# A four-layer cross-attention kernel: key norms by a power on GpSimd, idle products in an attention, and expert gate and up products in halves

## The reference, cut to what matters

```
# layer 1 (the second), attention, per head, window of 64 keys back
scores = q . k ; e = exp(scores - max) ; ctx = (e / sum(e)) @ v ; out = ctx @ o_w.T + o_b
# layer 1, feed-forward: 16 routed experts and a shared one (as two more), n = 448 tokens
gu   = einsum('nc,ech->neh', xf, gate_up_w)       # 128 -> 128 gate, 128 up
h    = silu(gate) * up
out  = einsum('neh,ehc->nec', h, down_w)          # 128 -> 128
moe  = einsum('ne,nec->nc', w_full, out)          # top 2 of 16, sigmoid gates
# layer 2 (the third), attention: keys of 1500 context rows, 8 heads of 64
k = k / max(sqrt(sum(k*k)), 1e-12) * k_scale
```

## Time and profile before

| | |
|---|---|
| median of 3 runs | 826.67 us (825.04 to 827.05) |
| the profiled execution, its own time | 825.94 us |
| its span | 824.1 us |
| granted TensorE clock, mean over the span | 0.943 |
| TensorE busy | 735.4 us (89%) |
| VectorE busy | 615.2 us (75%) |
| ScalarE busy | 438.3 us (53%) |
| GpSimd busy | 347.0 us (42%) |

### The profile page before, as it was taken

The page is one execution under the profiler, slowest core; times in us unless marked ns, Lnnn a source line. Parts: engine busy times, 40 slices in busy tenths (PEclk is TensorE's granted clock), DMA queues, the critical chain, the costliest instruction groups (busy, mean ns, idle before and its releaser), DMA issues.

```text
span 824.1 us, 15426 instructions
## 1 busy us (share of the span) xinstructions
PE 735.4 (89%) x5468; PEld 469.1 (57%) x5468; DVE 615.2 (75%) x1297; ACT 438.3 (53%) x739; POOL 347.0 (42%) x283
## 2 busy tenths in 40 slices
PE   3799999997886978998899999998899999898997
PEld 3577787776544465663455555563346666653443
DVE  4779999998878765567565566658689999516786
ACT  2656667677484433435444545432127776743674
POOL 0665555561523501640677787740242211102464
PEclk8999999999998878999999999999859999999999
DMA  8267767532424512206022333007736678101520
GB/s 208 75 205 252 252 198 227 173 117 72 98 67 131 160 51 76 86 29 177 3 79 78 104 100 101 6 10 103 128 71 131 124 126 165 37 2 64 180 78 12
DMA packets 50645, 89.71 MB, mean 109 GB/s; under 512 B 17427, under 2 KB 34779, under 8 KB 50099
## 3 DMA queue, kind: packets, MB, share of 16 engines
q1 hardware_dynamic: 50578, 88.83, 39.8%
HBM read 63.29 MB, written 25.52 MB: 108 GB/s over the span
## 4 chain that ended last, share of the span: by engine, by line
PE 29%; DVE 17%; POOL 2%; ACT 2%; issue 2%; DVEq 0%; POOLq 0%; ACTq 0%
DVE arena L2516 11%; PE ps L1165 9%; PE ps L1155 7%; PE ps L1334 3%; PE ps L1348 2%; DVE arena L1898 2%; POOL arena L1820 2%; PE ps L1270 2%; PE ps L1259 1%; ACT arena L1647 1%; PE ps L1201 1%; PE ps L1242 1%; PE ps L1313 1%; PE ps L1171 1%; PE ps L768 1%
## 5 line engine op out<-in xcount | busy, mean ns | idle before, releaser
L2516 DVE TENSOR_REDUCE arena<-ps 112x1 f32<-112x500 f32 x192 | 114.6, 670 | 9.0 <-PE ps L1242 9.0
L1820 POOL TENSOR_TENSOR arena<-arena 125x448 f32<-125x448 f32 x96 | 109.2, 1137 | 24.6 <-ACT arena L1606 20.7
L1898 DVE TENSOR_TENSOR arena<-ps,arena 128x448 f32<-128x448 f32 (+7 forms) x139 | 80.8, 612 | 37.5 <-ACT arena L1564 18.3
L1647 ACT ACTIVATE arena<-ps 125x896 f32<-125x896 f32 x96 | 87.2, 917 | 23.5 <-PE ps L1259 23.4
L1165 PE MATMUL ps<-arena 125*128 125x448 f32 (+1 forms) x208 | 97.2, 548 | 2.0 <-ACT arena L1606 1.5
L1606 ACT ACTIVATE arena<-arena,kbias 125x448 f32<-125x448 f32 x96 | 63.6, 668 | 65.4 <-DVE arena L1898 47.9
L1898 DVE TENSOR_TENSOR arena<-ps,rn 125x448 f32<-125x448 f32 x96 | 59.2, 618 | 47.0 <-PE ps L1155 42.1
L843 PE MATMUL ps<-w_k2h,arena 128*125 128x512 f16 x288 | 69.4, 392 | 11.6 <-ACT arena L1416 10.4
L1155 PE MATMUL ps<-arena 128*125 128x448 f16 (+3 forms) x312 | 76.5, 354 | 1.2 <-DVEq L1909 1.1
L1155 PEld LDWEIGHTS ps<-arena 128*125 128x125 f16 (+1 forms) x312 | 40.1, 133 | 54.8 <-issue 41.8
L1416 ACT ACTIVATE arena<-ps 125x512 f32<-125x512 f32 x96 | 55.4, 598 | 12.4 <-PE ps L843 9.8
(11 more groups left out here) (323 smaller groups left out, 1462.7 us busy)
## 6 DMA issues: line engine op xcount, KB each, us to landing
arena<-in_ctxT SPq DMA_DIRECT2D x8, 750.0 KB, 9.3
d_cln<-arena SPq DMA_DIRECT2D x8, 750.0 KB
d_clnT<-arena SPq DMA_DIRECT2D x8, 750.0 KB
d_k<-arena SPq DMA_DIRECT2D x24, 250.0 KB
d_v<-arena SPq DMA_DIRECT2D x24, 250.0 KB
arena<-d_clnT SPq DMA_DIRECT2D x8, 750.0 KB
arena<-in_ctx SPq DMA_DIRECT2D x8, 672.0 KB
arena<-d_cln SPq DMA_DIRECT2D x8, 672.0 KB
```

The lines of the kernel that those rows point to most:

```text
L1647: act.activation(p3[t % 2].rearrange("p (k h) q -> p k (h q)", k=2), ps[0:KP, 2 * (t % 2):2 * (t % 2) + 2, 0:8 * S], ACT.Exp).then_inc(l3_ ...
L1820: ins = pool.tensor_tensor(psum2[p][0:rows], psum2[p][0:rows], pexp[(t + p) % 2][0:rows], ALU.add)
L1898: return dve.tensor_tensor(out, a, b, op)
L2516: dve.tensor_reduce(mx3[bn % 2][:, u % 2, u % 8 // 2, u // 8:u // 8 + 1], ps[0:TT, max_bank_of(bn, u), 0:500], AX.X, ALU.max).then_inc(l3_ ...
```

## The change

**Norms.** The square root on ScalarE and the reciprocal on VectorE go. In their place GpSimd raises all of `rn` to the power -0.5 in one instruction, between `remainders(22)` and `remainders(23)`. VectorE waits for it (`rn_rt`) just before the third layer's attention.

**Idle products.** Before `turn_probs1(3)` TensorE waits until VectorE has read the last scores and then issues `keep_clock(9, 1)`.

**Experts.** Gate and up products are made of halves: `wh1` holds the high part and the remainder of the six gate and up matrices of a group, `x1h` those of the activations. The casts of groups 0 and 1 stand on ScalarE before `probs1(3)`, the subtractions on VectorE behind `normalise1(3)`; those of groups 2 to 5 stand in the expert stage, once in three experts. Both parts of `x1h` are made after `xT`, ahead of the first gate product. `gate_up1` now runs two experts ahead of `down1`, with three PSUM pairs and three `ex1` and `h1` tiles. The weights of a group are laid out as all gates and ups, then all downs, and loaded in two transfers, of 384 and 192 KB, each as its part of the buffer is free. All loops of this stage are written out. The waits of the fourth layer on the shared semaphores are shifted by what the second layer now adds to them (`SPLITS1`, and three down loads for each buffer).

```diff
+GU1 = G1 * 2 * 128
+SPLITS1 = 7
...
+UP_BANKS1 = (3, 5, 1)
...
+        wh1, h1, ex1 = [], [xT2, xT3], [exs[0], exs[1]]
+        for p in range(2):
+            words = kblk[p].rearrange("p e h s -> p (e h s)")
+            wh1.append(words[:, 0:768].bitcast(F16).rearrange("p (w n) -> p w n", w=2))
+            (h1, ex1)[p].append(words[:, 768:768 + N])
+        x1h = kblk[0].rearrange("p e h s -> p (e h s)")[:, 768 + N:768 + 2 * N].bitcast(F16).rearrange("p (w n) -> p w n", w=2)
...
-            def load_experts1(g, p):
-                sp.dma_start(wex[p][:, 0:G1 * 3 * D], batch(io["L1_ex"], g)).then_inc(ex_ld[p], 16)
+            def load_gate_up1(g, p):
+                sp.dma_start(wex[p][:, 0:GU1], io["L1_ex"][g, :, 0:GU1]).then_inc(ex_ld[p], 16)
+
+            def load_down1(g, p):
+                sp.dma_start(wex[p][:, GU1:G1 * 3 * D], io["L1_ex"][g, :, GU1:G1 * 3 * D]).then_inc(ex_ldd[p], 16)
...
-            with sp.Fori(0, E1 // G1 // 2 - 1) as i:
-                for p in range(2):
-                    g = 2 * i + p
-                    sp.wait_ge(ex_dn, G1 * (g + 1))
-                    load_experts1(g + 2, p)
+            sp.wait_ge(ex_split, 2)
+            for p in range(2):
+                load_gate_up1(2 + p, p)
+            for g in range(E1 // G1 - 2):
+                sp.wait_ge(ex_dn, G1 * (g + 1))
+                load_down1(g + 2, g % 2)
+                if g + 4 < E1 // G1:
+                    sp.wait_ge(ex_split, g + 4)
+                    load_gate_up1(g + 4, g % 2)
...
             for i in range(NT):
+                if i == NT - 1:
+                    pe.wait_ge(l1_sr, NT)
+                    keep_clock(9, 1)
                 turn_probs1(i)
                 if i + 2 < NT:
...
-            def w1(k, group, col):
-
-                return wex[group][:, D * (3 * k + col):D * (3 * k + col) + D]
-
-            def gate_up1(s, loads):
-
-                if s % G1 == 0:
-                    pe.wait_ge(ex_ld[s // G1 % 2], 16 * loads)
+            def gate_up1(e):
+
+                g, at = e // G1, e % G1 * 2 * D
+                pe.wait_ge(ex_split, 3 if g < 2 else g + 2)
+                if e > 2:
+                    pe.wait_ge(ex_h, e - 1)
                 for m in range(2):
-                    mm = pe.matmul(ps[0:D, 2 + 2 * (s % 2) + m, 0:N], w1(s % G1, s // G1 % 2, m), xT,
-                                   start=True, stop=True)
+                    for n, (w, a) in enumerate(((0, 0), (0, 1), (1, 0))):
+                        mm = pe.matmul(ps[0:D, UP_BANKS1[e % 3] - 1 + m, 0:N], wh1[g % 2][:, w, at + D * m:at + D * m + D],
+                                       x1h[:, a, :], start=(n == 0), stop=(n == 2))
                 mm.then_inc(ex_gu, 1)
...
-            def expert1(turn, s, more=True):
-                e = 2 * G1 * turn + s
-                if more:
-
-                    pe.wait_ge(ex_h, e + 1)
-                    gate_up1(s + 1, turn + 1 + (s + 1) // (2 * G1))
+            def down1(e):
+                g = e // G1
+                if e % G1 == 0:
+                    pe.wait_ge(ex_ldd[g % 2], 16 * (g // 2 + 1))
                 pe.wait_ge(ex_w, e + 1)
                 pe.wait_ge(ex_h, e + 2)
+                at = GU1 + e % G1 * D
                 for t in range(NT):
-                    mm = pe.matmul(ps[0:TT, 6 + s % 2, D * t:D * t + D],
-                                   (xT2, xT3)[s % 2][:, TT * t:TT * t + TT], w1(s % G1, s // G1 % 2, 2),
-                                   start=True, stop=True)
+                    mm = pe.matmul(ps[0:TT, 6 + e % 2, D * t:D * t + D], h1[e % 3][:, TT * t:TT * t + TT],
+                                   wex[g % 2][:, at:at + D], start=True, stop=True)
                 mm.then_inc(ex_dn, 1)
 
-            gate_up1(0, 1)
+            gate_up1(0)
             pe.wait_ge(lk_taken, 24 - IN_TURNS)
             pe.wait_ge(lv_taken, 24 - IN_TURNS)
-            with pe.Fori(0, E1 // (2 * G1) - 1) as i:
-                for s in range(2 * G1):
-                    expert1(i, s)
-            for s in range(2 * G1):
-                expert1(E1 // (2 * G1) - 1, s, more=s < 2 * G1 - 1)
+            gate_up1(1)
+            pe.wait_ge(to_act, 1)
+            for e in range(E1):
+                if e + 2 < E1:
+                    gate_up1(e + 2)
+                down1(e)
...
-            act.wait_ge(rn_sq, 1)
-            rn_flat = rn[:, :, :, :].rearrange("p b t h -> p (b t h)")
-            act.activation(rn_flat, rn_flat, ACT.Sqrt).then_inc(rn_sd, 1)
...
+            def split_hi1(g):
+                act.wait_ge(ex_ld[g % 2], 16 * (g // 2 + 1))
+                if g > 1:
+                    act.wait_ge(ex_gu, G1 * (g - 1))
+                act.copy(wh1[g % 2][:, 0, :], wex[g % 2][:, 0:GU1]).then_inc(ex_hi, 1)
+
             for i in range(NT):
+                if i == NT - 2:
+                    act.wait_ge(l1_s, NT)
+                    split_hi1(0)
+                    split_hi1(1)
...
+            act.wait_ge(operand, OPERAND["latentsT"] - 2)
+            act.copy(x1h[:, 0, :], xT).then_inc(ex_hi, 1)
+
+            def silu1(e):
                 act.wait_ge(ex_gu, e + 1)
-                act.activation(exs[p], ps[0:D, 2 + 2 * p, 0:N], ACT.Silu).then_inc(ex_act, 1)
-
-            silu1(0, 0)
-            silu1(1, 1)
-            act.wait_ge(to_act, 1)
-            act.activation(sm16[:, 6], sm16[:, 0], ACT.Sigmoid).then_inc(from_act, 1)
-            with act.Fori(1, E1 // 2) as i:
-                for p in range(2):
-                    silu1(2 * i + p, p)
+                act.activation(ex1[e % 3], ps[0:D, UP_BANKS1[e % 3] - 1, 0:N], ACT.Silu).then_inc(ex_act, 1)
+
+            for e in range(E1):
+                silu1(e)
+                if e == 1:
+                    act.wait_ge(to_act, 1)
+                    act.activation(sm16[:, 6], sm16[:, 0], ACT.Sigmoid).then_inc(from_act, 1)
+                if e % G1 == 0 and 1 < e // G1 + 1 < E1 // G1:
+                    split_hi1(e // G1 + 1)
...
-            remainders(22, 23)
+            remainders(22)
+            pool.wait_ge(rn_sq, 1)
+            rn_flat = rn[:, :, :, :].rearrange("p b t h -> p (b t h)")
+            pool.tensor_tensor(rn_flat, rn_flat, nhalf[0:KP, 0:1].broadcast_to([KP, B * KT * H8]), ALU.pow)\
+                .then_inc(rn_rt, 1)
+            remainders(23)
...
-                if i == 2:
-
-                    dve.wait_ge(rn_sd, 1)
-                    ch.step(dve.reciprocal(rn_flat, rn_flat))
                 normalise1(i)
+
+            def split_lo1(g):
+                dve.wait_ge(ex_hi, g + 1 if g < 2 else g + 2)
+                tt(wh1[g % 2][:, 1, :], wex[g % 2][:, 0:GU1], wh1[g % 2][:, 0, :], ALU.subtract).then_inc(ex_split, 1)
+
+            split_lo1(0)
+            split_lo1(1)
...
+            dve.wait_ge(ex_hi, 3)
+            dve.wait_ge(operand, OPERAND["latentsT"] - 2)
+            tt(x1h[:, 1, :], xT, x1h[:, 0, :], ALU.subtract).then_inc(ex_split, 1)
...
-            def hidden1(e, p):
+            def hidden1(e):
                 dve.wait_ge(ex_act, e + 1)
-                tt((xT2, xT3)[p], ps[0:D, 3 + 2 * p, 0:N], exs[p], ALU.mult).then_inc(ex_h, 1)
+                tt(h1[e % 3], ps[0:D, UP_BANKS1[e % 3], 0:N], ex1[e % 3], ALU.mult).then_inc(ex_h, 1)
...
-            weigh(0, 0, wts[:, :, 0:1], 0)
-            hidden1(2, 0)
-            weigh(1, 1, wts[:, :, 1:2], 0)
-            with dve.Fori(1, E1 // 2 - 1) as i:
-                for p in range(2):
-                    e = 2 * i + p
-                    hidden1(e + 1, 1 - p)
-                    weigh(e, p, wts[:, :, bass.ds(e, 1)], 0)
-            hidden1(E1 - 1, 1)
+            for e in range(E1 - 2):
+                weigh(e, e % 2, wts[:, :, e:e + 1], 0)
+                hidden1(e + 2)
+                if e % G1 == 1 and e // G1 + 2 < E1 // G1:
+                    split_lo1(e // G1 + 2)
...
+            dve.wait_ge(rn_rt, 1)
...
+    all1 = np.concatenate([experts1, np.stack(shared1)]).reshape(-1, G1, D, 3 * D)
...
-        "L1_ex": np.concatenate([experts1, np.stack(shared1)]).reshape(-1, G1, D, 3 * D).transpose(0, 2, 1, 3)
-        .reshape(-1, D, G1 * 3 * D),
+        "L1_ex": np.concatenate([all1[:, :, :, 0:2 * D].transpose(0, 2, 1, 3).reshape(-1, D, G1 * 2 * D),
+                                 all1[:, :, :, 2 * D:].transpose(0, 2, 1, 3).reshape(-1, D, G1 * D)], axis=2),
```

More of the change, by code:

```diff
@@ L449, in build @@
         acc_full, acc_used = sem("kv_sums_full"), sem("kv_sums_used")
-        rn_sq, rn_sd = sem("l2_key_squares"), sem("l2_key_norms")
+        rn_sq, rn_rt = sem("l2_key_squares"), sem("l2_key_norms")
         dve_s, pool_s = sem("dve_steps"), sem("pool_steps")
@@ L634, in _ @@
                     sp.wait_ge(lv_full, 16 - IN_TURNS + 1)
-                    load_experts1(0, 0)
+                    load_gate_up1(0, 0)
+                    load_down1(0, 0)
                 if u == 19:
                     sp.wait_ge(lv_full, 19 - IN_TURNS + 1)
-                    load_experts1(1, 1)
```

(28 more changed lines are left out.)

## The result

The changed kernel takes 918.80 us (median of 4 runs, 918.04 to 923.27), the kernel before 826.86 (4 runs): a ratio of 1.112, 95% interval 1.109 to 1.115. I had forecast 817.0 us, in a range from 812.5 to 823.0. What came is the rival with the long power. The profiled execution took 918.84, its span is 917.1 us, against 825.94 and 824.1 before.

What follows compares the result with a forecast made beforehand. TensorE bounds the experts; at the attention's end low clock and reciprocal end together. Attention -5.2, contention +0.4, experts -4.8 sum to -9.6: 825.94 becomes 816.3, with the median 0.73 above it 817.0 us; range 812.5 to 823.

Steps and rivals of the forecast that it cites:

- the rival with the long power: GpSimd's power outlasts the free time, delaying `remainders(23)` and `rsqrt`: 845 us at 50 us, 953 at 157; chance 0.20.
- the power on GpSimd: Power of 768 columns on GpSimd from 289.8 us, expected to take 16 to 18 us, inside the free time.
- The bound from above: Upper limit on the GpSimd power's length: 0.204 us a column from the 4-column power, 157 us for 768 columns.
- The 7.7 us: Estimate of the GpSimd power from the skill's page: 768 x 12 cycles at 1.2 GHz, inside the free time.
- Nearest to the elementwise rows: Choice of the GpSimd power's price between the bounds: about 0.02 us a column, 16 to 18 us.
- Free time: GpSimd's queue from 289.8 us until `remainders(23)` is due at 311.3: 21.5 us free, each further one costs one.
- Contention: VectorE's two-input subtraction at 296.78 us slowed beside the GpSimd power: 0 to 0.84 us lost, 0.4 taken.
- Attention: End of the attention, up to the layernorm: high clock and no reciprocal on VectorE gain 5.2 us.
- the clock falls all the same: Rival: TensorE's clock falls at gaps of some 1.2 us waiting for `normalise1(2)` and `normalise1(3)`; 819 to 821.5 us; chance 0.12.
- Its first case: The clock falls at 300 us: the attention gains only 0.1 us and the result is about 821.5 us.
- Experts: Expert stage: gate and up from halves, 0.35 us less per expert, less the start's cost: 4.8 us gained.
- VectorE as the experts' bound: Rival: VectorE's work keeps the experts' old 2.37 us, the stage loses 0.6 us: 822.5 us; chance 0.06.

Runs made afterwards that it cites:

- power_96: The changed kernel with GpSimd's power on 96 of the 768 columns, the other 672 multiplied by 1e-4 instead; 819.46 us.
- power_640: The changed kernel with GpSimd's power on 640 of the 768 columns, the others multiplied by 1e-4 instead; 897.11 us (1 run).
- act_power: The changed kernel with the norms' root and reciprocal in one ScalarE activation, no power on GpSimd; 818.55 us.
- spread_reciprocals: The changed kernel without the power: ScalarE's square root as before, VectorE's reciprocal cut by batches, seven of eight parts in the third layer; 818.42 us.

## Why the prediction was wrong

**The step that failed: the term of the sum "the power on GpSimd", 16 to 18 us.** It took 123.6. The mechanism was right, and stood among the rivals with its formula; its size, and with it its chance of 0.20, was not. I had two rows, a power of 4 columns at 1.03 us and elementwise work at 2.0 ns a column, and took most of the small power for a start that is paid once. It is the other way: per column the power costs 0.159 us, and at that price 0.64 of the small one's 1.03 us are its four columns. The bound from above, 0.204 us a column from the only power in the trace, was 1.3 times too high; my 0.02 was 8 times too low. The 7.7 us that the prediction estimates beside this value is 16 times too low for this power. "Nearest to the elementwise rows" was the wrong choice: the row with the same function was the nearer one, though it has few columns, since what GpSimd does for a power is not what it does for a product.

*Free time* 21.5 us: 24.8 measured in power_96. Right in place and mechanism (L1760 and L1744 behind it).

*Contention* +0.4, at most 0.84: 75.7 us on that one subtraction. The bounds were taken from multiplications of GpSimd beside VectorE, and a multiplication is over in 2 us; the bound should have been the power's own length. It cost nothing in the total here only because the queue held longer: after the release the attention needed 19 us, which ended 20.5 before the power did. In power_640 the same slack is 0.4 us.

*Attention* -5.2: -3.5 in act_power, -1.9 in spread_reciprocals and power_96. The reason is the rival "the clock falls all the same", between 303 and 307, with 1.7 of the 5.2 lost in act_power and 3.3 in the other two; with the clock held the term is 5.4. The rival's chance of 0.12 was too low: it happened in the trace of every kernel without the extra idle products. Its first case was mis-added besides: 5.1 of 5.2 lost is 817.0 + 5.1 = 822.1, not 821.5; nothing here hangs on it.

*Experts* -4.8: -4.0. The period is right (2.02). The start cost more, since the clock is low there: in act_power the first 18 gate and up products take 5.27 us, and three times 1.15 would be 3.45; in the kernel before the stage began at 1.00. In the changed kernel, after 23 us without TensorE, it gained only 2.3.

*Sum without the power's excess*: forecast 817.0; act_power 818.6, spread_reciprocals 818.4, power_96 819.5. *VectorE as the experts' bound* didn't come.

## What to carry to other kernels

Before a function is moved to an engine that has spare time, find its price per column there, from a row with that function; few columns bound it better than another function with many. If no row decides, the forecast belongs between the bounds, and a bound that lies beyond the free time is to be taken as a likely case. Here ScalarE did for 768 columns in 0.84 us what cost GpSimd 123.6.

An engine with nothing to do has a queue all the same: what counts isn't its idle time but when its next instruction is due.

Of two limits that end together (here the low clock and the reciprocal), taking away one gives little or nothing; try them together before discarding either.

## What the runs showed of the hardware

- A GpSimd power costs 0.159 us a column, on a line from 96 to 768 columns, in one instruction or in eight.
- A VectorE subtraction with two inputs in SBUF was held for 76.95 and 76.73 us beside powers of 768 and 640 columns, until 84 us after their start, and not at all beside 512, 384, 96 or eight times 96. A `tensor_scalar` of 4 columns was held to the end of the powers of 768 and 640 columns (20.66 and 0.59 us) and took 0.17 beside 512, 384 and eight times 96. Why there is a difference between more than 512 columns and fewer, and why the `tensor_scalar` is held to the end where two-input subtractions pass, stays open. What a hold alone would cost, with nothing queued behind the power, wasn't tried.
- The granted clock fell to 0.50 behind a gap of 1.47 us between products, ahead of one of 1.35 (act_power), or before a first gap of 1.44 us was over (spread_reciprocals), and stayed at 1.00 when both gaps were filled with idle products. Which of the two has to be filled wasn't tried.
